# Moving the first batch's maxima into the query stage, and interleaving the last residual sums

## The reference, cut to what matters

```python
def _L1_xattn_ref(hidden_q, kv_c, Wq, w_kc_q, w_kc_kv, W_qr, W_kr, Wo):
    q = (hidden_q @ Wq.T) ... @ w_kc_q @ W_qr        # 16 heads
    kv_rope = rope(kv_c)                             # 1500 rows of 64
    scores = q_r . (kv_rope @ W_kr)                  # per head
    attn = softmax(scores)
    ctx_c = attn @ kv_rope
    return (ctx_c @ w_kc_kv) @ Wo.T
def _moe_forward(...):                               # layer 3
    routed = expert_of(row)(x * sigmoid(gate))
    shared = silu_mul(x @ shared_gate_up) @ shared_down
    return routed + shared
```

## Time and profile before

| | us |
|---|---|
| median of 3 runs | 1624.12 |
| lowest, highest | 1620.94, 1625.83 |
| the profiled execution: its own time | 1622.73 |
| its span, first to last instruction | 1620.9 |
| TensorE busy in the span | 1525.7 (94%) |
| VectorE busy | 892.3 (55%) |
| GpSimd busy | 691.4 (43%) |
| ScalarE busy | 658.1 (41%) |

### The profile page before, as it was taken

One profiled execution on the slowest core, in us unless ns is written; L12 is line 12 of the kernel. 1 busy time (PEld: TensorE's weight loads), 2 busy tenths in 40 slices (PEclk: granted clock), 3 DMA queues, 4 the chain that ended last, 5 costly groups with the idle time before them and its releaser, 6 DMA issues. The chain is left out here.

```text
span 1620.9 us, 39525 instructions
## 1 busy us (share of the span) xinstructions
PE 1525.7 (94%) x17104; PEld 1222.2 (75%) x17104; DVE 892.3 (55%) x1624; ACT 658.1 (41%) x955; POOL 691.4 (43%) x506
## 2 busy tenths in 40 slices
PE   6898899999999999878998999999999999898998
PEld 3584688888888877666666888888888778746465
DVE  4950576666656626875546655555565153377212
ACT  3544244444444443552013444444444434244221
POOL 5414664465445100633966643654451026270101
PEclk9999799999999999998998999999999999999999
DMA  8016565654563203214025646545541030152402
GB/s 240 2 25 138 118 153 128 141 119 107 117 153 73 67 27 89 95 74 106 0 58 123 150 106 139 117 93 118 136 91 29 15 108 1 44 205 77 148 23 62
DMA packets 66461, 154.47 MB, mean 95 GB/s; under 512 B 14972, under 2 KB 44220, under 8 KB 65424
## 3 DMA queue, kind: packets, MB, share of 16 engines
q1 hardware_dynamic: 65520, 150.10, 37.0%
q0 software_dynamic: 768, 1.84, 0.4%
HBM read 87.51 MB, written 5.51 MB: 57 GB/s over the span
## 5 line engine op out<-in xcount | busy, mean ns | idle before, releaser
L1624 DVE TENSOR_REDUCE latent_psW<-latent_psW 128x1 f32<-128x500 f32 x654 | 418.2, 682 | 234.5 <-PE latent_psW L1519 234.1
L1602 ACT ACTIVATE latent_w<-latent_psS 125x896 f32<-125x896 f32 x384 | 351.7, 919 | 429.7 <-PE latent_psS L1537 426.1
L1547 PEld LDWEIGHTS latent_psO<-latent_val,latent_w 125*64 125x64 f32 x10752 | 324.1, 138 | 25.5 <-issue 11.9
L1547 PE MATMUL latent_psO<-latent_val,latent_w 125*64 125x65 f32 x10752 | 339.8, 223 | 0.6 <-issue 0.6
L1536 PE MATMUL latent_psS<-latent_qA,latent_kA 128*125 128x448 f32 x768 | 290.8, 379 | 3.9 <-DVE latent_qB L1640 2.4
L1537 PE MATMUL latent_psS<-latent_qB,latent_kB 128*125 128x448 f32 x768 | 283.3, 369 | 0.0
L1519 PE MATMUL latent_psW<-latent_kA,latent_qA 128*128 128x500 f32 x654 | 214.5, 398 | 3.1 <-DMA latent_qA<-latent_qh 2.4
L1536 PEld LDWEIGHTS latent_psS<-latent_qA,latent_kA 128*125 128x125 f32 x768 | 143.8, 187 | 31.2 <-ACT latent_w L1602 4.6
L1537 PEld LDWEIGHTS latent_psS<-latent_qB,latent_kB 128*125 128x125 f32 x768 | 144.0, 188 | 19.8
L1519 PEld LDWEIGHTS latent_psW<-latent_kA,latent_qA 128*128 128x128 f32 x654 | 124.8, 191 | 19.5 <-DVE latent_psW L1624 5.0
L946 POOL TENSOR_TENSOR latent_rawT<-latent_rawT,latent_ropeT 128x1000 f32<-128x1000 f32 x48 | 110.8, 2334 | 34.1 <-DMA latent_rawT<-in_ctx_cols 22.3
(11 more groups left out here) (411 smaller groups left out, 2222.5 us busy)
## 6 DMA issues: line engine op xcount, KB each, us to landing
latent_qA<-latent_qh SPq DMA_DIRECT2D x128, 112.0 KB, 2.5
latent_rawT<-in_ctx_cols SPq DMA_DIRECT2D x32, 375.0 KB, 5.8
latent_rawT<-in_ctx_cols SPq DMA_DIRECT2D x64, 187.5 KB, 6.4
latent_raw<-in_ctx SPq DMA_DIRECT2D x32, 375.0 KB
latent_kA<-latent_high SPq DMA_DIRECT2D x32, 375.0 KB, 4.0
latent_kB<-latent_high SPq DMA_DIRECT2D x32, 375.0 KB, 5.4
latent_kA<-latent_rawT SPq DMA_DIRECT2D x32, 375.0 KB, 6.2
experts_wgu<-in_L_gu SPq DMA_DIRECT2D x8, 1024.0 KB, 15.0
```

What stands on the lines that cost most here:

```text
L1547: last = pe.matmul(sums[r:r + 64, c, :], w[t % ROUND][:, queries_of(c, r):queries_of(c, r) + 64], val[b % 2][:, t, :], start=(t == 0 and c ...
L1602: act.activation(w[t % ROUND][:, :].rearrange("p (h n) -> p h n", h=2), psS[0:KP, t % 2, :, 0:GH], ACT.Exp).then_inc(exp_done, 1)
L1624: dve.tensor_reduce(bank[:, THIRD + j:THIRD + j + 1], bank[:, 0:THIRD], mybir.AxisListType.X, ALU.max).then_inc(max_ready, 1)
```

## The change

Five things change together.

1. `first.load` (keys and tables of the first pair) is issued by SP in `top8_ffn`, one stage earlier; its buffers are placed there.
2. In `queries_plain` GpSimd starts with `rope_keys(0)`, behind a wait for VectorE's last normalised tile, then does `fill`, `rope_rows`, `low_keys`, clears `mx` and `qB0`, makes the low queries of batch 0 and does `rope_keys(1)`. SP loads the second pair's columns once the fold is over, stores the keys, then copies `qA0` and `qB0`.
3. The query groups run over the heads first, then over the halves of the tokens. `high_keys` stands behind the third copy, the split of batch 0's queries behind the eighth. Behind the eleventh group TensorE waits for the keys and `qA0`, and then issues the 21 products of the first batch's maxima in portions of 3, 3, 3, 4, 4, 4 behind groups 11 to 16. VectorE reduces them in this stage. The attention stage starts with the transposition.
4. In `queries_roped` the first batch's queries are split and copied at the end of the stage; the 21 products stay in the attention stage of layer 2. In both layers `keep_busy` falls from 18 to 6.
5. In `experts_ffn` the routed sum of tile t-2 follows the shared sum of tile t, and each output store waits for its routed sum.

```diff
@@ top8_ffn
+            @block.sync
+            def _(sp):
+                first.load(sp)
@@ LatentFirst
+    def empty_queries(self, pool, norm):
+        pool.wait_ge(norm.turned_ready, NT)
+        pool.memset(self.mx[:, :, :], 0.0).then_inc(self.empty, 1)
+        pool.wait_ge(self.empty, 1)
+        pool.memset(self.qB[64:128, :].bitcast(F32), 0.0).then_inc(self.empty, 1)
+        pool.wait_ge(self.empty, 2)
+    def store_queries(self, sp):
+        GH = HP * S
+        self.store(sp)
+        sp.wait_ge(self.qh_ready, 1)
+        for e in range(2):
+            for r in range(2):
+                sp.dma_start(self.qA[r * 64:r * 64 + 64, e * GH:(e + 1) * GH].bitcast(F32),
+                             self.qh[e * 64:e * 64 + 64, :].bitcast(F32)).then_inc(self.qA_came[0], 16)
+        sp.wait_ge(self.ql_ready, 1)
...
@@ queries_plain
             def _(sp):
-                first.load(sp)
-                first.store(sp)
+                sp.wait_ge(rest.a_done, HP // 2)
+                first.load_columns(sp, 2)
+                first.load_columns(sp, 3)
+                first.store_queries(sp)
             def _(pool):
+                pool.wait_ge(norm.xn_ready, NT)
+                first.rope_keys(pool, 0)
                 first.fill(pool)
-                first.rope_keys(pool, 0)
                 first.rope_rows(pool, 0)
                 first.low_keys(pool, 0)
+                first.empty_queries(pool, norm)
+                first.low_queries(pool, q)
+                first.rope_keys(pool, 1)
             def _(pe):
...
+                def score_for_max(x):
+                    j, m = x // 3, x % 3
+                    wait_from(pe, first.max_ready, x - 5)
+                    pe.matmul(max_bank(x), first.qA[:, j * 128:(j + 1) * 128], first.kA[0][:, first.part(m)],
+                              start=True, stop=True).then_inc(first.max_scores, 1)
+                x = 0
+                for n in range(2 * HP):
+                    queries(n)
+                    if n == 2 * HP - 6:
+                        pe.wait_ge(f["taken"], HP)
+                        pe.wait_ge(first.kA_came[0], 48)
+                        pe.wait_ge(first.qA_came[0], 64)
+                    for _ in range(max(0, n - 2 * HP + 7) and (3 if n < 2 * HP - 3 else 4)):
+                        score_for_max(x)
+                        x += 1
             def _(act):
-                    j, h = n // 2, n % 2
+                    h, j = n // HP, n % HP
...
-                    if n == 3:
+                    if n == HP - 1:
+                        act.wait_ge(q_taken, HP)
+                        first.high_queries(act, q)
+                    if n == 2:
                         first.high_keys(act, 0)
             def _(dve):
                 norm.vector(dve)
+                for x in range(MAX):
+                    dve.wait_ge(first.max_scores, x + 1)
+                    dve.tensor_reduce(parts[:, x % 3, x // 3:x // 3 + 1], max_bank(x), X, ALU.max).then_inc(first.max_ready, 1)
+                dve.wait_ge(first.max_ready, MAX)
+                dve.wait_ge(first.empty, 2)
+                dve.tensor_reduce(first.mx[:, 0, 0:QTL], parts[:, :, :].rearrange("p m j -> p j m"), X, ALU.max).then_inc(first.maxima_ready, 1)
@@ queries_roped
-                first.store(sp)
+                first.store_queries(sp)
...
+                    if group == 2 * QUADS - 2:
+                        act.wait_ge(q_taken, 2 * group + 2)
+                        first.high_queries(act, q)
...
+                    if n == 18:
+                        first.empty_queries(pool, norm)
+                first.low_queries(pool, q)
@@ latent_attention
-                store_queries(0)
+                sp.dma_start(mask[:, :, :], d["max_mask"].rearrange("p (c n) -> p c n", n=128)).then_inc(mask_came, 16)
                 store_queries(1)
-                sp.dma_start(mask[:, :, :], d["max_mask"].rearrange("p (c n) -> p c n", n=128)).then_inc(mask_came, 16)
-                store_low_queries(0)
-                n.load_columns(sp, 2)
-                n.load_columns(sp, 3)
+                if not n.maxima_made:
+                    n.load_columns(sp, 2)
+                    n.load_columns(sp, 3)
...
-                keep_busy(pe, g, psO[:, 0:128], 18)
-                pe.wait_ge(cleared, 6)
-                for x in range(NX):
-                    score_for_max(0, x, alone=True)
+                keep_busy(pe, g, psO[:, 0:128], 6)
+                if not n.maxima_made:
+                    for x in range(NX):
+                        score_for_max(0, x, alone=True)
@@ experts_ffn
-                    sp.wait_ge(x_done, NT + t + 1)
+                    sp.wait_ge(sum_ready, t + 1)
...
+                for t in range(NT):
+                    take_shared(t)
+                    if t >= 2:
+                        take_routed(t - 2)
+                take_routed(NT - 2)
+                take_routed(NT - 1)
```

More of the change, by code:

```diff
@@ L731, in top8_weights, with top8_ffn @@
     return w
-def top8_ffn(nc, g, weights, later):
+def top8_ffn(nc, g, weights, later, first):
     E = 64
@@ L876, in __init__ @@
         self.rawT_came = [a.sem(f"rawT_came{u}") for u in range(2)]
+        self.qA_came = [a.sem(f"qA_came{u}") for u in range(3)]
+        self.qB_came = [a.sem(f"qB_came{u}") for u in range(2)]
+        self.qh_ready, self.ql_ready, self.max_scores, self.max_ready, self.maxima_ready, self.empty = (
+            a.sem(n) for n in ("qh_ready", "ql_ready", "max_scores", "max_ready", "maxima_ready", "empty"))
+        self.nc, self.g, self.layer, self.maxima_made = nc, g, layer, False
         self.kA_came = [a.sem(f"kA_came{u}") for u in range(3)]
@@ new lines, in store_queries @@
+    def store_queries(self, sp):
+        GH = HP * S
+        self.store(sp)
[5 more added lines that the diff above has]
+        sp.wait_ge(self.ql_ready, 1)
+        for e in range(2):
+            sp.dma_start(self.qB[0:64, e * GH:(e + 1) * GH].bitcast(F32),
+                         self.ql[e * 64:e * 64 + 64, :].bitcast(F32)).then_inc(self.qB_came[0], 16)
@@ L994, in plain_weights @@
     w = Weights(nc, g, "q1_w")
+    w.folding = ExitStack()
+    kept, w.a = w.a, Alloc(nc, w.folding, "q1_fold", g.arena)
     both = lambda name, n: [d[name].rearrange("r (j e i) -> r j e i", j=HP, e=2)[:, :, e, :] for e in range(2)]
@@ L1001, in plain_weights @@
     w.wq = w.put([128, NH, C], (None, d["L1_wq"].rearrange("k (h n) -> k h n", h=NH)))
+    w.a = kept
     w.wkv = w.put([128, NH, DC], (None, d["L1_wkv"].rearrange("k (h n) -> k h n", h=NH)))
@@ L1104, in queries_plain @@
         q_done, q_taken = a.sem("q_done"), a.sem("q_taken")
+        w.folding.close()
+        first.place_queries()
+        first.maxima_made = True
+        MAX, QTL = NH * S * 3 // 128, NH * S // 128
+        parts = a.sb("parts", [128, 3, QTL])
+        max_bank = lambda x: (norm.turned, ps_z, ps_y)[x % 6 // 2][:, x % 2, 0:first.THIRD]
         with nc.Block() as block:
@@ L1126, in _, with queries @@
                 pe.wait_ge(rest.a_ready, HP // 2)
-                n = 0
-                for j in range(HP):
-                    for h in range(2):
-                        if n >= 2:
-                            pe.wait_ge(q_taken, n - 1)
-                        for c in range(CC):
-                            last = pe.matmul(ps_q[:, n % 2, 0:HALF], aw[:, j, c, :, :], g.xnT[:, c, h * HALF:(h + 1) * HALF],
-                                             start=(c == 0), stop=(c == CC - 1))
-                        last.then_inc(q_done, 1)
-                        n += 1
+                def queries(n):
+                    h, j = n // HP, n % HP
+                    if n >= 2:
+                        pe.wait_ge(q_taken, n - 1)
+                    for c in range(CC):
+                        last = pe.matmul(ps_q[:, n % 2, 0:HALF], aw[:, j, c, :, :], g.xnT[:, c, h * HALF:(h + 1) * HALF],
+                                         start=(c == 0), stop=(c == CC - 1))
+                    last.then_inc(q_done, 1)
+                def score_for_max(x):
[13 more added lines that the diff above has]
+                        x += 1
             @block.scalar
@@ L1239, in queries_roped @@
         ctx.callback(w.kept.close)
+        first.place_queries()
+        first.place_loads()
         first.place()
@@ L1657, in _ @@
                     dve.memset(lanes[0][:, 0:1], 0.0).then_inc(lanes_summed, 1)
-                dve.wait_ge(cleared, 6)
-                for x in range(NX):
-                    maximum(0, x, alone=True)
-                maxima(0, alone=True)
+                dve.wait_ge(n.empty, 2)
+                if not n.maxima_made:
+                    for x in range(NX):
+                        maximum(0, x, alone=True)
+                    maxima(0, alone=True)
                 take_maxima(0)
@@ L1736, in _, with latent_layer @@
                 norm.vector_tile(dve, NT - 1)
```

(13 more changed lines are left out.)

78 lines of the change are left out of this document (50 added, 28 removed).

## The result

The median went from 1622.35 us (1616.98 to 1627.09, 20 runs taken beside the changed kernel's) to **1617.64 us** (1613.68 to 1620.41, 20 runs): ratio 0.9969, 95% interval 0.9960 to 0.9978, so 3.6 to 6.5 us faster. The forecast was 5.6 us, at 1618.5. Ratios are of fast runs: of the first experiments' executions, two of the kernel before and two of the end alone were slow (1667 us to 6.5 ms) and are left out of them.

A forecast was written before the change was run, and what follows sets the result against it. TensorE, busy 94% of the span, was taken as the bound, with time to win where it idles or is clocked low. Gains 0.8 + 2.4 + 2.4 = 5.6 gave 1624.1 - 5.6 = 1618.5 us, range 1612.5 to 1623.5.

The forecast's parts named there:

- the third, layer 1: Layer 1 query stage to score products: scores start at 181.9 instead of 182.68, a gain of 0.8 us.
- GpSimd's chain: Layer 1 query stage: rotation starts at 125.6, low keys end at 150.5 instead of 152.5.
- SP and the landing: Layer 1: SP issues key copies, then `qA`, which lands at 161; TensorE idles 10.6 us from 150.4.
- The half clock: Layer 1, behind the wait for `qA`: TensorE runs at half clock for 5 us, reductions end at 177.6.
- I am wrong if the clock behind it is full: Sign against the forecast: full TensorE clock behind the layer 1 wait for `qA`.
- the rival in which the clock holds: Layer 1: clock holds or returns at once; layer 1 gives 4.6, total 1613.1 us; chance 0.22.
- Full-clock reductions, 12.4 us: Layer 1: at full clock VectorE's 21 reductions at 0.59 us take 12.4 us, more than TensorE's work.
- the first rival: The clock holds or comes back at once in layer 1, 1613.1 us in all; chance 0.22.
- The start of attention: Layer 1: stage starts at 178.1, mask lands 2.4 us after issue, score products start at 181.9 instead of 182.68.
- Layer 2: Start of layer 2's attention: queries land by 850.3, products start at 851.8 instead of 854.28, 2.4 us gained.
- The end: End of the program: three routed sums remain after the last shared sum instead of eight, 2.4 us gained.

The follow-up runs named there:

- the end alone: The kernel before with only the experts_ffn change, shared and routed sums interleaved at the end; 1620.87 us, ratio 0.9987.
- the other profile of this layer 1: The changed kernel with the old order put back in layer 2, layer 1 and the end as changed; 1619.79 us, ratio 0.9982 to the kernel before.
- the filler: The changed kernel with 38 filler products ahead of TensorE's wait for the first batch's queries in layer 1; 1614.31 us, ratio 0.9948 to the kernel before.

## Why the prediction was right

The time and two of the three terms came out about as worked out; the third, layer 1, was off by about its own small size, which is less than the profiles of one kernel differ by.

*The level.* The gain was 4.7 instead of 5.6, yet the time came out 0.9 below the forecast. The kernel before stood at 1624.12 in the three runs that the forecast started from, and at 1622.35 in the 20 beside the changed kernel. These 1.8 us are scatter of that kernel and no part of the working; on the later base the forecast would have been 1616.8. So that the time came so close to 1618.5 is partly luck.

*GpSimd's chain.* Right. The low keys were to end 34.6 us after the stage's start (115.86 to 150.5); they ended 34.8 after it (114.69 to 149.5). `high_keys` ran at 139.32 with no stall, and query groups were 1.5 us apart.

*SP and the landing.* Right in the sum. From the low keys to the landing 10.5 was worked out; 11.0 was measured. The key issues took 4.2, as said; the `qA` issues took 1.2 each, not 0.8, which they took where only one copy stood ahead. The wait was 9.6 instead of 10.6 because the folds took 1.4 us longer than in the trace of before, so that TensorE came to it later; in the other profile of this layer 1, with the folds at 4.46, it was 11.05. The Trainium skill, "DMA: Bandwidth & Descriptors", "Queues, rings and completion order", was cited for the ring's order; by that rule the landing follows the copies ahead of it, and the trace agrees: 11.0 us behind four key copies, 5.9 behind one.

*The half clock.* Right. About 5 us at half speed behind the wait were assumed; the clock was 0.50 from 160 to 165 and 0.91 after; in the other profile it was 0.50 for four us behind the 11.05. "I am wrong if the clock behind it is full" did not happen; the rival in which the clock holds was only made true by the filler. From the landing to the end of the reductions 16.6 us were worked out, and 17.0 measured. What was taken from the Trainium skill, "TensorE: Matmul & The Clock Gate", "HAM oscillation — how this bites in real kernels", was that bursts behind a transfer wait start at the low clock. After 11.05, 9.60, 5.34 and 4.62 us the traces agree; after 0.89 us, and after the 2.04 behind the filler, nothing was lost. Between these a profile can go either way: in that of the end alone the clock fell behind the stall of 2.16 us in the old layer 1, in that of before it held behind 2.35.

*Full-clock reductions, 12.4 us.* Wrong: 13.8. The step took VectorE as the bound and left out the 0.34 us gaps between portions, in which it waits for TensorE. It did not reach the forecast, since the half clock covered it, but it did reach the first rival: layer 1 at full clock would have given 3.2 by it, not 4.6.

*The start of attention.* The step that failed in size. The mask was to land 2.4 us after its issue and took 3.6; the masked write ended at 182.7 instead of 181.8, and the scores came at 182.78 instead of 181.9. With that, layer 1 gave 0.1 by the first query product instead of **0.8**; the repeated profiles (48.2 to 48.7 against 46.7 to 49.6) leave it at nothing that can be told. In the eight other traces in which the mask is loaded there it landed in 2.1 to 2.5 us, the second profile of this layer 1 among them. So the 3.6 belongs to this one execution, and no run shows its cause; without it layer 1 would have shown some 1.2 more (an estimate from these landings). The first scores ran at half clock for some 3.7 us (182.78 to 186.5) instead of the 6.3 that the forecast kept from before; in the three profiles of the old layer 1 it was 3.1, 5.8 and 6.2, so that is not the change either.

*Layer 2.* The first maximum products started 3.2 us after the last query product instead of 5.6: the **2.4** as worked out. The stage change took 1.89 us of idle instead of 0.89, a bit over the 0.7 said. The scores gained only 2.1, because the first three maximum products, behind a third of the filler, took 1.58 us instead of 0.92, and VectorE began 0.85 us after the first of them instead of 0.58.

*The end.* 2.5 by the distance and 2.1 by the ratio of the run with that part alone, beside **2.4**. Three routed sums stayed, no gather was late.

*What the profiled spans add.* They differ by 8.6 us, 3.9 more than the medians. The trace of the changed kernel is 3.1 shorter from 638.8 to the last query products of layer 2, a stretch in which the change touches only the end of the query stage. From 638 to 700 the clock was 0.97 in the profile of before and 1.00 in the other; what made the rest is not shown.

## What to carry to other kernels

A step moved forward is only as early as what stands in front of it in each list: here a copy waited for three others that nobody needed yet, and behind 5.7 us of GpSimd's work that could wait. Read both lists down to the transfer, and put first what the bound engine waits for: that turned a gain of 5 us into one of 18. Price a wait as its idle time plus the slow work behind it, and size a term under 1 us from several profiles or not at all. Measure a stage from its start and also from a point inside it: here the folds in between shifted the inner point by 1.4 us and made two good forecasts look off.

## What was not expected of the hardware

- The clock also fell in some profiles before any wait of this change. The 32 fold products behind the four turns of the normalised tiles, which stand 0.3 to 0.5 us apart, took 4.46 us in five of eleven profiles and 5.6 to 5.9 in six. From 128 to 134 us the clock was 1.00 in the profile of before and 0.72 in that of the changed kernel. Both happened with the old layer 1 stage and with the new one.
- Behind waits of 4.6 and 5.3 us stood some 3 us of half clock (four products 2.6 to 2.7 us instead of 1.67), behind 9.6 some 5, and behind 11.05 some 4. A short stall can do it too: in the profile of the end alone the 40 query products behind the stall of 2.16 us took 17.00 us, and the clock was 0.68 from 144.6 to 150; in the profile of before they took 15.30 behind 2.35 us, at a clock of 1.00.
- The mask of 112 KB landed 2.1 to 2.5 us after its issue in eight profiles, and 3.6 in one.
